# Output projections begun ahead of the last head group, one root for four norms, and row maxima moved behind the value projection

## What is computed

```python
x = x + cross_attention(layernorm(x), ctx, rope positions)   # @ W_o + b_o at its end
x = x + causal_self_attention(layernorm(x), rotated q and k) # @ w_o at its end
x = x + moe_ffn(layernorm(x))  # 32 experts, the best 4 of each row, and a shared part
```

## Time and profile before

| | us |
|---|---|
| median of 3 executions | 1864.06 |
| lowest and highest | 1862.05, 1866.74 |
| profiled execution, its own time | 1859.28 |
| its span in the trace | 1858.0 |
| mean granted clock of PE in it | 0.924 |
| PE, DVE, ACT, POOL busy | 1627.6, 1218.5, 1079.1, 678.9 |

### The profile page before, as it was taken

The page is one execution under the profiler, slowest core; times in us unless marked ns, Lnnn a source line. Parts: engine busy times, 40 slices in busy tenths (PEclk is TensorE's granted clock), DMA queues, the critical chain, the costliest instruction groups (busy, mean ns, idle before and its releaser), DMA issues.

```text
span 1858.0 us, 25396 instructions
## 1 busy us (share of the span) xinstructions
PE 1627.6 (88%) x9532; PEld 990.2 (53%) x9532; DVE 1218.5 (66%) x2695; ACT 1079.1 (58%) x1269; POOL 678.9 (37%) x321
## 2 busy tenths in 40 slices
PE   5578888888788884799999999999988888999998
PEld 4455555555455552433444434344475556888886
DVE  5456667666667677699999899899876344222222
ACT  3356666666556655687888888888741234333332
POOL 3156656655666654599100000000030013434442
PEclk7888999999989996899999999999996789999999
DMA  4644445555444544743455445444222002434341
GB/s 156 179 125 125 125 130 156 156 170 139 125 125 125 150 147 126 174 114 91 114 126 125 114 114 131 119 114 114 69 77 76 1 1 98 136 117 133 121 129 57
DMA packets 91435, 219.40 MB, mean 118 GB/s; under 512 B 10876, under 2 KB 11132, under 8 KB 86448
## 3 DMA queue, kind: packets, MB, share of 16 engines
q1 hardware_dynamic: 90912, 216.98, 42.4%
q10 hardware_dynamic: 400, 0.79, 0.2%
HBM read 144.22 MB, written 55.65 MB: 108 GB/s over the span
## 4 chain that ended last, share of the span: by engine, by line
PE 59%; DVE 13%; issue 8%; DMA 6%; SPq 5%; ACT 5%; POOL 4%; POOLq 0%; DVEq 0%; ACTq 0%
PE PS L114 27%; PE PS L640 12%; PE PS L672 10%; DMA cs<-kr 6%; SPq L67 5%; PE PS L414 4%; DVE rel L427 4%; DVE khd L394 2%; DVE acc L663 1%; PE PS L682 1%; ACT P L646 1%; POOL kr L384 1%; POOL kr L381 1%; POOL cs L382 1%; PE PS L833 1%
## 5 line engine op out<-in xcount | busy, mean ns | idle before, releaser
L646 ACT ACTIVATE P<-PS 128x1024 f32<-128x1024 f32 x512 | 481.8, 1038 | 98.1 <-PE PS L640 80.6
L663 DVE TENSOR_TENSOR acc<-acc,P 128x2048 f32<-128x2048 f32 x216 | 507.7, 2415 | 34.3 <-ACT P L646 34.2
L427 DVE CUSTOM_DVE_ANT_0 rel<-PS,rel 128x256 f32<-128x256 f32 x1024 | 362.8, 420 | 161.7 <-PE PS L414 161.4
L420 ACT ACTIVATE rel<-PS 128x1024 f32<-128x1024 f32 x256 | 262.8, 1027 | 172.7 <-PE PS L414 167.4
L414 PE MATMUL PS<-khd,qh 32*128 32x256 f32 x2048 | 143.0, 356 | 140.5 <-DVE khd L394 108.5
L672 PE MATMUL PS<-P,qe 128*32 128x512 f32 x2048 | 258.7, 604 | 0.7 <-ACT on L677 0.7
L414 PEld LDWEIGHTS PS<-khd,qh 32*128 32x128 f32 x2048 | 87.3, 204 | 238.1 <-ACT kr L513 93.0
L114 PE MATMUL PS<-R,Wh 128*128 128x512 f32 x512 | 182.9, 441 | 9.7 <-ACT kr L513 8.7
L114 PE MATMUL PS<-Wh,R 128*128 128x512 f32 x512 | 185.3, 419 | 2.1 <-ACT cs L518 2.1
L108 POOL TENSOR_TENSOR El<-We,Eh 128x1536 fp32r<-128x1536 f32 x36 | 126.0, 3500 | 166.3 <-ACT Eh L105 166.2
L108 POOL TENSOR_TENSOR w3l<-qk,w3h 128x2048 fp32r<-128x2048 f32 x2 | 9.1, 4561 | 482.2 <-ACT w3h L105 482.2
(11 more groups left out here) (213 smaller groups left out, 2490.3 us busy)
## 6 DMA issues: line engine op xcount, KB each, us to landing
khd<-kscr SPq DMA_DIRECT2D x129, 256.0 KB, 4.0
We<-in_w_e SPq DMA_DIRECT2D x36, 768.0 KB, 5.8
y<-in_y SPq DMA_DIRECT2D x16, 1024.0 KB, 6.4
cs<-kr SPq DMA_DIRECT2D x128, 128.0 KB, 6.7
vscr<-cs SPq DMA_DIRECT2D x16, 1024.0 KB, 4.8
kscr<-khd SPq DMA_DIRECT2D x16, 1024.0 KB, 8.6
kscr<-kl SPq DMA_DIRECT2D x16, 1024.0 KB, 7.2
qe<-vscr SPq DMA_DIRECT2D x64, 256.0 KB, 4.7
```

The costliest lines, as they stand in the source:

```text
L420: return AC.sig(nc.scalar.activation(rel[i][:, :, :, :], PS[:, 2 * b:2 * b + 2, :].rearrange("p j (t n) -> p j t n", t=2), ACT.Relu))
L427: m = DV.sig(nc.vector.tensor_tensor_reduce(out=rel[i][:, j, t, :], in0=PS[:, 2 * b + j, t * 256:(t + 1) * 256], in1=rel[i][:, j, t, :], s ...
L646: expm[s, pr] = spfree[b] = AC.sig(nc.scalar.activation(P[s % 4][:, 2 * pr:2 * pr + 2, :], PS[:, 2 * b:2 * b + 2, :], ACT.Exp, scale=SCALE))
L663: accm[s] = DV.sig(nc.vector.tensor_tensor(a[:, :, :], a[:, :, :], P[s % 4][:, :, :], ALU.add))
```

## The change

At start-up b_o is loaded early, spread over all partitions, and POOL adds it to X in four additions. The first third of w_qkv has a tile of its own (`w3q`) and is loaded ahead of the first rope swap. At the end of cross attention the first three k-tiles of the output projection run for all four query tiles (`out_first`), and the last group is divided, split and multiplied by query tile (`out_last`). `add_and_measure` adds the four tiles to X, takes their statistics, and makes one root and one reciprocal for the four; `normalized` scales, transposes and splits. The low parts of w_qkv move from POOL to DVE. The value product has no units inside; the eight units of group 0 follow it, each with `warm(4, 7)`, behind a wait for V2's eviction. The units of groups 1 to 3 lie in groups 0 to 2, and `shifts(g + 1)` at the end of the group. The wo splits move from group 2 to group 1. The self attention's end takes the same form as that of cross attention. Tables of Exp and Sqrt are asked for early by small instructions.

```diff
+        PL.wait(t_bo, t_n)
+        for t in range(4):
+            t_xb = PL.sig(nc.gpsimd.tensor_tensor(X[:, t, :], X[:, t, :], kr[0][:, 0, :], ALU.add))
         SP.wait(t_wqs)
...
         load_cs(1)
+        t_w3 = [l_w3[0].dma(SP, w3q[:, :, :], w_qkv[:, :, 0:512])]
         PE.wait(ev, t_wks, t_wvs)
-        AC.wait(t_wks, t_wvs)
+        AC.wait(t_wks, t_wvs, t_xb)
...
-        dfree, t_ot = outputs(3)
-        PE.wait(expm[total - 1, 0], expm[total - 1, 1])
-        warm(26, 0)
+        def out_first(ready, free):
+            PE.wait(free)
+            for k in range(3):
+                PE.wait(ready[k])
+                for qt in range(4):
+                    out_product(qt, k, k == 0, False)
+        def out_last(o, rc_, den, bias, ready):
+            pm = []
+            for qt in range(4):
+                cols = slice(qt * 128, (qt + 1) * 128)
+                DV.wait(ready)
+                m_ = DV.sig(nc.vector.reciprocal(rc_[:, cols], den[:, cols]))
+                DV.wait(m_)
+                m_ = DV.sig(nc.vector.tensor_tensor(o[:, cols], o[:, cols], rc_[:, cols], ALU.mult))
+                AC.wait(m_)
+                hi_ = AC.sig(nc.scalar.activation(R[0][:, 3, cols], o[:, cols], ACT.Identity, bias=bias))
+                DV.wait(m_, hi_)
+                m_ = DV.sig(nc.vector.scalar_tensor_tensor(R[1][:, 3, cols], o[:, cols], bias, R[0][:, 3, cols].bitcast(F32),
+                                                           ALU.add, ALU.subtract))
+                PE.wait(m_, hi_)
+                pm.append(PE.sig(out_product(qt, 3, False, True)))
+            return pm
+        def add_and_measure(pm):
+            for qt in range(4):
+                DV.wait(pm[qt])
+                m_ = DV.sig(nc.vector.tensor_tensor(X[:, qt, :], X[:, qt, :], PS[:, qt, :], ALU.add))
...
+            AC.wait(m_)
+            m_ = AC.sig(nc.scalar.activation(rstd[:, :], mv[:, :, 1], ACT.Sqrt, bias=epst[:, 0:1]))
+            DV.wait(m_)
+            return DV.sig(nc.vector.reciprocal(rstd[:, :], rstd[:, :]))
...
+        out_first([t_wos, t_wos, t_ot], [expm[total - 1, 0], expm[total - 1, 1]])
+        AC.wait(onm[3])
+        AC.sig(nc.scalar.activation(ex[:, 0:1], epst[:, 0:1], ACT.Sqrt))
+        pm = out_last(on[1], rec, DEN, cst[:, 19:20], [final[3], onm[3]])
+        t_rstd = add_and_measure(pm)
         barrier()
...
+        w3m = [w3_high(0)]
+        t_xT = normalized(xn2, R[0], R[1], t_rstd)
+        t_ws = [w3_low(0, w3m[0])]
...
-        t_ws = [split_w3(0)]
-        t_xT, t_used = project(bo, xn2, R[0], R[1])
-        t_ws += [split_w3(1), split_w3(2, t_used)]
+        w3m += [w3_high(1), w3_high(2)]
...
+        t_ws += [w3_low(1, w3m[1]), w3_low(2, w3m[2])]
...
-                              lambda k: w3h[2][:, k, :], lambda k: w3l[2][:, k, :], 4, between=between_values)
+                              lambda k: w3h[2][:, k, :], lambda k: w3l[2][:, k, :], 4)
...
-        for i, x_ in enumerate(early):
-            row_maxima(*x_, i % 4 if i < len(early) - 4 else i % 3)
+        PE.wait(pairfree[3])
+        for i, (qt, hp) in enumerate((qt, hp) for qt in (3, 2, 1, 0) for hp in range(2)):
+            row_maxima(0, qt, hp, i % 3)
+            warm(4, 7)
         shifts(0)
-        late = {g: [(g + 2, qt, hp) for qt in (0, 1, 2, 3) for hp in range(2)] for g in range(2)}
+        rest = {g: [(g + 1, qt, hp) for qt in (3, 2, 1, 0) for hp in range(2)] for g in range(3)}
...
-                if j == 1 and g < 3:
-                    shifts(g + 1)
-                if g < 2:
-                    row_maxima(*late[g][2 * j], 2)
+                if g < 3:
+                    row_maxima(*rest[g][2 * j], 2)
...
+                    if j == 3:
+                        shifts(g + 1)
-                if g == 2:
+                if g == 1:
                     t_wos.append(split(qk[0][:, j, :], R[2][:, j, :], R[3][:, j, :], t_wo, t_v, PL))
...
-        t_xT, _ = project(None, xn2, R[0], R[1])
+        out_first([[t_wos, t_at[0]], t_at[1], t_at[2]], [pairfree[0], pairfree[1]])
+        pm = out_last(oc[1], rc[1], PS[:, 7, :], zero[:, 0:1], last_o)
+        t_rstd = add_and_measure(pm)
+        warm(8, 6)
+        t_xT = normalized(xn2, R[0], R[1], t_rstd)
```

More of the change, by code:

```diff
@@ L195, in build @@
         cs2 = sbc("cs2", [128, 2, 4, 512])
+        w3q = sbc("w3q", [128, 4, 512])
+        l_w3 = [lane(f"l_w3{i}") for i in range(3)]
         two, sbt = stack()
@@ L254, in build @@
         t_n = [normalize(X, xn, t, t_x) for t in range(4)]
+        t_bo = lane("l_bo").dma(SP, kr[0][:, 0, :], A["b_o"].to_broadcast([128, 512]))
+        w_qkv = A["w_qkv"].rearrange("(k p) n -> p k n", p=128)
         t_q = [transpose_tile(xn, xh, xl, t, t_n[t]) for t in range(4)]
@@ new lines, in normalized @@
+        def normalized(xn, hT, lT, ready):
+            tr, done = [], []
+            for qt in range(4):
+                DV.wait(ready)
+                m_ = DV.sig(nc.vector.tensor_scalar(xn[:, qt, :], X[:, qt, :], mv[:, qt, 0:1], rstd[:, qt:qt + 1],
+                                                    ALU.subtract, ALU.mult))
+                PE.wait(m_, t_const)
+                for c in range(4):
+                    ins = nc.tensor.transpose(PS[:, 4 + qt, c * 128:(c + 1) * 128], xn[:, qt, c * 128:(c + 1) * 128], ident[:, :])
+                tr.append(PE.sig(ins))
+            for qt in range(4):
+                cols = slice(qt * 128, (qt + 1) * 128)
+                done.append(split(PS[:, 4 + qt, :].rearrange("p (c n) -> p c n", c=4), hT[:, :, cols], lT[:, :, cols], tr[qt]))
+            return done
@@ L728, in build @@
         QK = [[sbq(f"QK{i}{w_}", [128, 4, 512], F32R) for w_ in "hl"] for i in range(2)]
[L730 to L749, removed]
         sz, sbw = stack()
-        bo = W[0][:, 0:512]
         xn2 = sbw("xn2", [128, 4, 512])
         qk = [sbw(f"qk{i}", [128, 4, 512]) for i in range(2)]
-        w3 = [qk[0], qk[1], V2]
+        w3 = [w3q, qk[1], V2]
         xsw = [xn2, sbw("xsw", [128, 4, 512])]
@@ L766, in build, with w3_high, w3_low @@
         w3l = [sbv(f"w3l{i}", [128, 4, 512], F32R) for i in range(2)] + [R[3]]
-        t = l_c.dma(SP, bo, A["b_o"].to_broadcast([128, 512]))
-        DV.wait(t)
         t_mask = l_m.dma(SP, mask, A["c_mask"])
-        l_w3 = [lane(f"l_w3{i}") for i in range(3)]
-        t_w3 = [l_w3[p_].dma(SP, w3[p_][:, :, :], A["w_qkv"].rearrange("(k p) n -> p k n", p=128)[:, :, p_ * 512:(p_ + 1) * 512])
-                for p_ in range(3)]
+        t_w3 += [l_w3[p_].dma(SP, w3[p_][:, :, :], w_qkv[:, :, p_ * 512:(p_ + 1) * 512]) for p_ in (1, 2)]
+        def w3_high(p_):
+            AC.wait(t_w3[p_])
+            return AC.sig(nc.scalar.copy(w3h[p_][:, :, :], w3[p_][:, :, :]))
+        def w3_low(p_, m_):
+            DV.wait(t_w3[p_], m_)
+            return DV.sig(nc.vector.tensor_tensor(w3l[p_][:, :, :], w3[p_][:, :, :], w3h[p_][:, :, :].bitcast(F32), ALU.subtract))
+        for i in range(2):
+            t_mxz = PL.sig(nc.gpsimd.memset(mxz[i][:, :, :], 0.0))
+        w3m = [w3_high(0)]
+        t_xT = normalized(xn2, R[0], R[1], t_rstd)
+        t_ws = [w3_low(0, w3m[0])]
         AC.wait(t_ang2)
@@ L893, in build @@
         pairfree[2], pairfree[3] = evs[2][1], evs[2][3]
+        AC.wait(t_v)
+        AC.sig(nc.scalar.activation(rstd[:, 0:1], epst[:, 0:1], ACT.Exp))
         def shifts(g):
@@ L940, in values @@
             pfree[n] = m = PE.sig(ins)
-            if j == 3:
+            if j == 3 and g == 3:
+                AC.wait(m, t_at.get(g - 2))
+                c_ = AC.sig(nc.scalar.copy(oc[1][:, :], PS[:, 6, :]))
+                last_o.extend([m, c_])
+            elif j == 3:
                 AC.wait(m, t_at.get(g - 2))
@@ L971, in build @@
         values(15)
-        PE.wait(list(t_at.values()), t_wos)
-        t_xT, _ = project(None, xn2, R[0], R[1])
+        AC.sig(nc.scalar.activation(rstd[:, 0:1], epst[:, 0:1], ACT.Sqrt))
+        out_first([[t_wos, t_at[0]], t_at[1], t_at[2]], [pairfree[0], pairfree[1]])
[3 more added lines that the diff above has]
+        t_xT = normalized(xn2, R[0], R[1], t_rstd)
         barrier(l_e)
```

31 lines of the change are left out of this document (14 added, 17 removed).

## The result

The changed kernel took 1879.08 us (median of 5, 1871.74 to 1880.53) against 1863.77 for the kernel before: ratio 1.0072, 95% interval 1.0044 to 1.0099. A second series (last experiment) gave 1873.15 against 1863.72, ratio 1.0036, 1.0014 to 1.0059. So the change makes the kernel slower, by 9 to 15 us when the medians are subtracted and by 7 to 13 by the ratios. The profiled execution took 1879.87, 20.6 above that of before; that of the second series took 1877.42.

The account below looks back on a forecast made before the run. No engine bounds the kernel's end by itself; PE's three-part products are the longest piece, so stages were priced singly. +8.7 - 5.9 + 13.1 - 2.0 = +13.9 us, 1878 on the median; own range 1872 to 1886, overall 1861 to 1887.

Parts of the forecast that it names:

- Start-up: Start-up, to the first rope: POOL's b_o additions and the early w_qkv load cost +8.7 us (bounds +0.5 and +10.2).
- First projection: End of cross attention to the q, k products: rearranged projection and norm gain 5.0 us, about 2.7 after the lower clock.
- Value product and first units: Value projection to first score: PE idles, then units run at 1.2 GHz; first score 1433, -5.9 us with the step before.
- Groups: Self attention groups: groups 0 to 2 carry eight units each, group 3 none; +13.1 us (bounds +10.2 and +16).
- Tail: Second projection and norm, to the router: same rearrangement gains, -2.0 us (-3.0 to -0.5).
- Rival (a): Start-up hides its work: additions and load together cost only 0.5 to 2 us; 1869 to 1871 on the median; chance 0.14.
- (d): Both rearranged projections and norms gain nothing because DVE bounds both ends: +20.9 us, 1885; chance 0.06.
- Rival (b): First units: warm-ups lift PE to 2.4 GHz late; first score 1427, group 0 at 19.3; +2 us, 1866; chance 0.12.
- Rival (c): Value projection through groups: without the idle wait PE stays at 2.4 GHz; -9.5 us, 1854.5 on the median; chance 0.16.

Follow-up runs that it names:

- last experiment: The changed kernel unaltered, measured a second time beside the kernel before: median 1873.15 us, ratio 1.0036.
- e4: Changed kernel plus 32 warm-up instructions ahead of PE's wait for V's eviction, so PE does not idle there: median 1859.89 us, ratio 0.9998 to the kernel before.
- after: First profile of the changed kernel, against the kernel before; this profiled execution took 1879.87 us.
- e8: Changed kernel with 16 units behind V, 32 warm-ups ahead of them, none behind each, start-up additions and load moved into cross attention: 1847.37 us, 0.9917 to before.
- e1: Changed kernel with b_o loaded and added to X at key tile 8 of cross attention, not at start-up: median 1874.98 us, ratio 1.0107 to before.
- e3: Changed kernel without the warm(4, 7) behind each of the eight units after the value product: median 1862.20 us, ratio 1.0001 to the kernel before.
- e5: Changed kernel with units, shifts and wo splits back in their places of the kernel before: median 1858.50 us, ratio 0.9979 to the kernel before.
- e7: Changed kernel with 16 units of groups 0 and 1 behind V, no warm-ups, start-up additions and load moved into cross attention: 1843.99 us, 0.9898 to before.

## Why the prediction was right, step by step

The forecast, +13.9 or 1878 on the median, lies 1 us from the first result and 5 from the second, and its direction is that of both. In the profiles, from which the terms are read, the change cost 20.6 and 18.1, so that the median came out so near is in part luck. The terms:

- **Start-up, 8.7 forecast, 6.1 measured.** Both causes are real: 3.8 for the additions (4.9 forecast) and 2.3 for the load (3.8 with its issue). The additions cost less because DVE did not stand still beside them as it does beside one long subtraction: it took turns with them, and four steps lost 3.9 together. L269 took 1.66 where L263 had taken 4.98, but that older loss did not go away; it moved with y's low half to L277.
- **First projection, -5.0 forecast, -5.9 measured.** A tile of `out_last` took 2.11 (2.14 forecast), a tile's addition and statistics 1.55 (1.67). The q, k products lost 2.5 to the lower clock (24.6 against 22.1; 2.3 forecast).
- **Value product and first units, -5.9 with the step before, -7.6 measured.** PE's wait was 3.3 (3.7 forecast), the clock behind it 0.50, a unit 3.15 (3.2). Most hung on this step, and e4 shows its cause, the idle wait, to be the right one for the changed kernel. In before I had misread it: the clock had fallen ahead of the 5.85 of idling, not in it. Of two sets of three dense matmuls inside the value product, the second took 1.56 instead of 0.91, at the lower clock, and the idling began only at its end:

```profile
1400.83 0.91 PE L114 MATMUL PS<-R 128*128 128x512 f32 x3
...
1403.31 1.56 PE L114 MATMUL PS<-R 128*128 128x512 f32 x3
```

One more reading was too broad: I took the 0.50 of the old units as what units do, but with warm-ups and without a wait they hold 2.4 GHz (e4). The Trainium skill (TensorE: Matmul & The Clock Gate, Part 1) says that sustained activity releases the throttle; the units of after, busy for 24.9 of 25.6 us at 0.50, and those of e8, which lost the clock while busy, do not agree.

- **Groups, +13.1 forecast, +18.9 measured.** Group 0 came out at 25.0 (24.75). Groups 1 and 2 took 27.3 each (25.5) and group 3 took 16.3 (14.2). I had priced groups at the clock of the old group 1, 0.86; they ran at 0.69, 0.69 and 0.68. For group 3 that accounts for the difference: in e1 to e4 the same code ran it at 1.00 in 14.2 to 14.3. For groups 1 and 2 the mean clock alone does not: e3, for one, took 29.1 at 0.71, 25.4 at 0.80 and 14.3 at 1.00 for groups 1 to 3:

```profile
1446.30:1475.40 29.10, 22.91 (x180) 12.75 (x180) 11.17 (x11) 8.33 (x15) 3.81 (x3) 0.71 0.00 1
1475.40:1500.80 25.40, 20.24 (x180) 11.71 (x180) 11.17 (x11) 7.29 (x13) 1.29 (x1) 0.80 0.01 1
1500.80:1515.10 14.30, 11.35 (x161) 6.93 (x162) 5.04 (x4) 6.35 (x11) 0.00 (x0) 1.00 0.01 1
```

In all six profiles with this code (after twice, e1 to e4) groups 1 and 2 come to 54.5 or 54.6 together, 3.5 over the 51.0 that I forecast; what sets this was not settled. One wait in them is plain in after, and the prediction does not name it. At the head of group 1 the units' maxima stand on DVE behind the division of group 0 (L995), and PE idles 2.60 before the third unit:

```profile
1472.29 3.35 DVE L995 RECIPROCAL rc<-PS 128x512 f32<-128x512 f32 x1
...
1479.07 0.69 PE L885 MATMUL PS<-QK1h,QK0h 32*128 32x384 f32 x2 [2.60 <-DVE mxz L890]
```

Before, units met a division in group 1 only; after, they meet one in groups 1 and 2. That what the groups carry costs the bulk is shown by e5.

- **Tail, -2.0 forecast, -3.3 measured;** but the router, starting at 1.2 GHz, and what follows gave back 2.1 in both profiles of after, which stood in no term of the sum. Together -1.2. The seven steps listed for the tail add up to 23.4 and not to 23, so the term as worked out was -1.6. By the Trainium skill (TensorE: Matmul & The Clock Gate, Part 4: PE-mode transpose) the transposes ahead of the router do not count as busy in the same way. The router of after did begin at the lower clock. The profile of e3 does not agree: its 16 transposes began at the lower clock, as in after (3.58 against 3.68 us), and its router, with nothing else on PE in between, ran at the full one (0.62 for the first pair against 1.03).

The errors cancel in part: start-up 2.6 less, groups 5.8 more, projections 3.0 more gain, end 2.1 more loss. Rival (a) is refuted (both start-up causes show), (d) too. Rival (b) did not occur. Rival (c) named the right place and cause of the clock's fall. Its sum had a slip: a first score at 1422 is 1407.4 + 13.1 + 1.8 and so keeps the wait that its condition takes away; without the wait it would be 1418.6. And the groups do not keep the clock: they took 93.8 in e4 where (c) has 77.65, and e4 lies at 1860 rather than at 1854.5.

## What to carry to other kernels

Price dummy work, too, at the clock that it will run at. A unit with its eight warm-up instructions took 3.15 us at 1.2 GHz (after) and 1.75 at 2.4 (e4), of which the warm-ups were 2.02 and 1.11; without them it took 1.16 with its share of the shift, mostly at 1.2 (e7). Here dummy matmuls held the clock when no wait stood ahead of them (e4) and did not bring it back behind one (after), and even where they held it the stage was longer than without them. "Idle" engines are not free ones: POOL's additions, 5.0 long when alone, cost little beside a DVE with slack (tile 96), and nearly that length where DVE sets the pace (3.8 at start-up, 4.3 at tile 8).

## What the runs showed of the hardware that I had not expected

A 128x512 addition on POOL takes 1.26 us alone, 1.8 in a row of four beside DVE's angle steps (7.07), and 3.3 beside its running sums (13.14); the sums take 3.36 instead of 2.29. The clock can fall while PE is busy without a gap: in e8 from 1.00 to 0.50 within units of 32-row matmuls. The same run of units and warm-ups, with PE busy, stayed at the clock that it began with: 0.50 in after, 1.00 in e4. And in the kernel before, three dense matmuls between each two units had not raised it again.
